# Unread bf16 matmuls on TensorE behind norms, between thin row scores and at the waits at the end of attentions

## The chip, the cores and the metric

The kernel runs on one core of one Trainium2 chip. The metric is the device time of one execution in microseconds (us); smaller is better. The engines are TensorE (PE, matmul), VectorE (DVE), ScalarE (ACT), GpSimd (POOL) and SyncE (SP). They run side by side, each through its own list in order, and wait for one another by semaphores.

## What is computed

A stack of four levels on x (4 sequences of 512 tokens, 128 features), with a context of 77 tokens of 64 features. Each level adds a gated cross attention and a gated feed-forward part:

```python
x = x + tanh(g_xattn[0]) * L0_xattn(layernorm(x), ctx)   # 16 heads of 8
x = x + tanh(g_ffn[0])   * L0_ffn(layernorm(x))          # quantised MLP
x = x + tanh(g_xattn[1]) * L1_xattn(layernorm(x), ctx)   # self attention a1, cross attention a2, 16 heads of 32, an MLP behind each
x = x + tanh(g_ffn[1])   * L1_ffn(layernorm(x))          # causal self attention, 16 heads of 8, then 8 experts, one per token
x = x + tanh(g_xattn[2]) * L2_xattn(layernorm(x), ctx)   # one head
x = x + tanh(g_ffn[2])   * L2_ffn(layernorm(x))          # 4 experts, two per token
x = x + tanh(g_xattn[3]) * L3_xattn(layernorm(x), ctx)   # 16 heads of 8
x = x + tanh(g_ffn[3])   * L3_ffn(layernorm(x))          # attention over the 4 sequences, 8 experts
```

## The kernel before

Everything stands transposed: features on the 128 partitions, tokens along the free side. All levels but the last feed-forward part run in a loop of two turns (`TURNS`), and a turn treats two sequences, u = 0 and 1, at the same time. Matmuls are f32 but for a few in bf16; they write the 8 banks of PSUM (`PSB[b]`, 512 f32 columns each). Each engine has one hand-written list. `TENSOR.did(...)` counts a step of PE and `pe.wait_ge(*VECTOR[...])` waits for one of DVE; PE takes its matmuls strictly in the order written. So a matmul that waits holds up all behind it, and one that does not wait delays what stands behind it by its own length, unless that would have waited anyway.

Three functions of PE's list are touched.

`norm(tag, src, ready)` normalises over features. PE centres u = 0 and 1 (line 613), ACT squares both (L1555), PE takes the means (line 616), ACT makes the reciprocal deviation with Ln and Exp (L1558, L1560), DVE multiplies (L1879) and in most cases applies gain and offset (L1884). PE then waits for DVE. The tags in order of a turn are l0x, l1o, l1a, l1b, a1n3, l1c, l1d, a2n3, l1f, l1g, l2x, l2f, l3x.

`cross(tag, dh)` is the cross attention, with dh = 8 in l0x and l3x and dh = 32 in a2. First come eight pairs of row scores of u = 0 (`rowscores`, line 641: 32 of the 128 rows of the array each), each followed by a maximum on DVE (L1927), in a ring of three pairs of banks. The maxima are turned (line 654), then columns of scores (line 670), exponentials on ACT (L1574) and values (line 695) of both sequences are interleaved. With dh = 8 the end is `heads` (line 709: sums per head), a reciprocal on DVE, `inverses` (line 719), and behind it the output projection (`linear`, line 1002).

`attend_past` is the causal attention of l1f, in 32 pieces of four heads. It starts with row scores (line 881, with `diagonals`, line 887) of pieces 0 to 4, the suffix sums (line 918) and the turned maxima. The loop over m then does row scores of piece m + 6, column scores (line 912) of piece m and values (line 932) of piece m - 2. Towards the end PE spreads small tables (`spread_out`, line 953), sums per head (`heads`, line 945), takes the logits of the router (`logits`, line 1206), and the experts follow (lines 1236 and 1242, with DVE L2391 between them). For u = 1 the queries are made by ACT (L1743, step `"l1f q", 1`); in the kernel before PE waits for it only ahead of column score 1 and row score 16.

Of the kernel before, what the change touches and what calls it, by code (L numbers as in the profile page):

```python
# [116 lines left out]
def program(nc, xT, ctxT, const, packs, l2w, w1, w2, out, tables):  # L117
    ctx = ExitStack()
    with ctx:
# [7 lines left out]
        PSB = [ps[:, b, :] for b in range(8)]  # L127
# [7 lines left out]
        def aux(u):  # L135
            return PSB[6 + u]
# [17 lines left out]
        identb = sb("identb", [128, 128], BF16)  # L154
        w1q = sb("w1q", [128, 512], BF16)
# [60 lines left out]
        SCALAR = Steps(sem("scalar_steps"), tables[1])  # L216
# [390 lines left out]
        def _(pe):  # L607
            ident = K["ident"]

            def norm(tag, src, ready, dim=128):  # L610
                for u in U:
                    pe.wait_ge(*ready(u))
                    pe.matmul(lin(u), K["centre"], src(u), start=True, stop=True).then_inc(*TENSOR.did(tag, "c", u))  # L613
                for u in U:
                    pe.wait_ge(*SCALAR[tag, "sq", u])
                    pe.matmul(aux(u), K["mean"], sq[:, u, :], start=True, stop=True).then_inc(*TENSOR.did(tag, "v", u))

            def cross(tag, dh):

# [10 lines left out]
                def rowscores(u, a):  # L630
                    i, hf = a // 2, a % 2
                    x = cplace("R", u, a)
                    free(x)
                    if a == 0:
                        pe.wait_ge(*VECTOR[tag, "kv", u])
                        pe.wait_ge(*VECTOR[tag, "q", u])
                    for b in (0, 1):
                        c = 2 * hf + b
                        at = slice(32 * c, 32 * c + 32)
                        if dh == 8:  # L640
                            mm = pe.matmul(PSB[cbank(x) + b][:, 0:4 * KC], qT[at, u, 0, 128 * i:128 * i + 128],  # L641
                                           kt[at, u].rearrange("p k t -> p (k t)"), start=True, stop=True,
                                           tile_position=(32 * c, 0))
                        else:
                            mm = pe.matmul(PSB[cbank(x) + b][:, 0:4 * KC], qT[:, u, c, 128 * i:128 * i + 128],
                                           apart(u)[:, c], start=True, stop=True)
                    mm.then_inc(*TENSOR.did(tag, "R", u, a))

                def turned(u):
                    x = cplace("turned", u)  # L650
                    pe.wait_ge(*VECTOR[tag, "cut", u])
                    free(x)
                    for i in range(4):
                        mm = pe.transpose(PSB[cbank(x)].bitcast(BF16)[:, 128 * i:128 * i + 128],
                                          cut[:, i].rearrange("p c r -> p (c r)"), identb[:])
                    mm.then_inc(*TENSOR.did(tag, "turned", u))
# [43 lines left out]
                def heads(u, hf):  # L700

                    x = 34 + u
                    if hf == 0:
                        free_late(x)
                    pe.wait_ge(*SCALAR[tag, "kept", u, hf])
                    to = PSB[cbank(x)][:, 0:64].rearrange("p (i c k) -> p i c k", i=4, c=4)
                    source = (xn if hf == 0 else sq)[:, u, :]
                    for i in range(4):
                        mm = pe.matmul(to[:, i, :, 2 * hf:2 * hf + 2], source[:, 128 * i:128 * i + 128],
                                       eighths[:, :, 1 - hf, :], start=True, stop=True, skip_group_check=True)  # L710
                    mm.then_inc(*TENSOR.did(tag, "heads", u, hf))
# [4 lines left out]
                def inverses(u):  # L716
                    pe.wait_ge(*VECTOR[tag, "inv", u])
                    for i in range(4):
                        mm = pe.matmul(PSB[cbank(34 + u) + 1][:, 128 * i:128 * i + 128], rs[:, u, 128 * i:128 * i + 128], ident,
                                       start=True, stop=True)  # L720
                    mm.then_inc(*TENSOR.did(tag, "inverses", u))
# [2 lines left out]

                for a in range(8):
                    rowscores(0, a)
                turned(0)
                for a in range(8):
                    colscores(0, a)
# [17 lines left out]
                if dh == 8:  # L747
                    heads(1, 0)
                    inverses(0)
                    heads(1, 1)  # L750
                    inverses(1)
                    return
                for u in U:
                    pe.wait_ge(*VECTOR[tag, "inv", u])
                    for k in range(4):
# [3 lines left out]
                        for c in range(4):  # L759
# [3 lines left out]
                                           stop=True, tile_position=(0, 32 * c))  # L763
# [100 lines left out]
            def attend_past(token_values, logits):  # L864
# [19 lines left out]
                def diagonals(p, h):  # L884
                    x, lo = pplace(p, h), 128 * ktile_past(p)
                    for b in (0, 1):
                        mm = pe.matmul(PSB[pbank(x) + b][:, lo:lo + 128], identb[:], beyond[:], start=False, stop=True)  # L887
                    mm.then_inc(*TENSOR.did("l1f", "R", p, h))
# [49 lines left out]
                def heads(u, hf):  # L938

                    bank = 3 - 2 * u  # L940
                    pe.wait_ge(*(VECTOR["l1f", "raised", 7] if u == 0 else VECTOR["l1f", "later", 0]))
                    pe.wait_ge(*SCALAR["l1f", "kept", 2 * u + hf])
                    to = PSB[bank][:, 0:64].rearrange("p (i c k) -> p i c k", i=4, c=4)
                    for i in range(4):
                        mm = pe.matmul(to[:, i, :, 2 * hf:2 * hf + 2], kept_sums(2 * u + hf)[:, 128 * i:128 * i + 128],
                                       eighths[:, :, 1 - hf, :], start=True, stop=True, skip_group_check=True)
                    mm.then_inc(*TENSOR.did("l1f", "heads", u, hf))

                def spread_out(tag, u, bank):

                    pe.wait_ge(*VECTOR["l1f", tag, u])
                    for i in range(4):
                        mm = pe.matmul(PSB[bank][:, 128 * i:128 * i + 128], xn[:, u, 128 * i:128 * i + 128], ident, start=True,
                                       stop=True)
                    mm.then_inc(*TENSOR.did("l1f", tag, u))

                for p in range(5):
                    for c in range(4):
                        rowscore(p, c)
                        if c % 2:  # L960
                            diagonals(p, c // 2)
                    if p == 0:
                        token_values(1)
                for u in U:
# [6 lines left out]
                for m in range(34):  # L971
                    if m % 4 == 3 and m < 28:
                        turned((m + 1) // 4)
                    for g in range(4):
                        if g == 2 and m >= 2:
                            values(m - 2)
                        if m + 6 < 32:
                            rowscore(m + 6, g)
                        if m < 32:
                            colscore(m, g)  # L980
                        if m + 6 < 32 and g % 2:
                            diagonals(m + 6, g // 2)
                    if m == 28:
                        pe.wait_ge(*VECTOR["l1f", "max", 31, 1])
                        spread_out("e0", 0, 1)
                    if m == 29:
                        spread_out("e0", 1, 2)
                        heads(0, 0)
                        heads(0, 1)
                    if m == 31:  # L990
                        spread_out("inv", 0, 4)
                    if m == 32:
                        heads(1, 0)
                heads(1, 1)
                logits(0)
                spread_out("inv", 1, 2)

            def linear(tag, w, src, ready, rows=None):
                for u in U:
# [91 lines left out]
            with pe.Fori(0, TURNS) as t:  # L1091
# [110 lines left out]
                def logits(u):  # L1202
                    pe.wait_ge(*VECTOR["l1f o", u])
                    pe.wait_ge(*SCALAR["l1f", "exp", 31, 3])
                    for i in range(4):
                        mm = pe.matmul(aux(u)[:, 16 * i:16 * i + E1], x2[:, u, 128 * i:128 * i + 128], w["Wsw"],
                                       start=True, stop=True)
                    mm.then_inc(*TENSOR.did("l1f logits", u))
# [92 lines left out]
                for u in U:  # L1301
# [3 lines left out]
                    for c in range(2):  # L1305
                        mm = pe.matmul(scb(2 * u + c), w["rW1"][:, 128 * c:128 * c + 128], xn[:, u, :], start=True,
                                       stop=True)
# [38 lines left out]
                for u in U:  # L1346
                    pe.wait_ge(*VECTOR["l2f cwT", u])
                    pe.wait_ge(*VECTOR["l2f out", 2 * E2 - 2 + u])
                    for i in range(4):
                        pe.matmul(aux(u)[:, 128 * i:128 * i + 128], x2[:, u, 128 * i:128 * i + 128], ident, start=True,  # L1350
                                  stop=False)
# [1409 lines left out]
```

## Time and profile before

| | |
|---|---|
| median of 3 runs | 1945.53 us (1936.75 to 1956.92) |
| profiled execution | 1932.59 us, of which the span of the trace is 1930.5 us |
| mean granted TensorE clock | 0.87 of 2.4 GHz |
| busy: PE, DVE, ACT, POOL | 1643.6, 880.0, 715.9, 146.9 us |
| share of the chain that ended last: PE, DVE, ACT | 78%, 12%, 7% |
| DMA | 30.17 MB, 16 GB/s on average |

PE's clock is granted at one of two levels, 2.4 GHz (1.00) or 1.2 GHz (0.50); a value between them is a mean over a stretch that has both. "Idle before" of a PE row counts from the modelled end of the last matmul.

### The profile page before, as it was taken

The page shows a single profiled execution, that of the slowest core. Times are in us where ns is not written, and L with a number is a line of the kernel's source. Part 1 is how long each engine was busy: PE and PEld are TensorE (multiplying, and loading weights), DVE is VectorE, ACT ScalarE, POOL GpSimd, SP SyncE. Part 2 cuts the span into 40 slices and gives each one's busy share as a digit, 9 for nine tenths or more (in the row PEclk, how much of TensorE's full clock was granted, in tenths as well). Part 3 has the DMA queues.
Part 4 walks back from the last instruction along what each step waited for, and adds up shares of the span by engine and source line. Part 5 has one row for each costly group of instructions (what it writes and reads, how often), then busy time and mean ns, then how long its engine had stood idle before and what let it go on. Part 6 is the DMA issues. An engine that isn't in the chain of part 4 may idle for free.

```text
span 1930.5 us, 22528 instructions
## 1 busy us (share of the span) xinstructions
PE 1643.6 (85%) x9068; PEld 762.3 (39%) x9068; DVE 880.0 (46%) x1746; ACT 715.9 (37%) x1267; POOL 146.9 (8%) x207
## 2 busy tenths in 40 slices
PE   5748999989899989997648999989899989988487
PEld 2323333332344536633323323332343436543274
DVE  4474664253456353324474663353456352337312
ACT  2333455324435225232332455323445125243133
POOL 0000011100012000000000111100012000002232
PEclk9768899989989699956768999989999689889688
DMA  4000000000000100000000000000000100002241
GB/s 178 1 1 0 1 2 1 1 1 1 0 1 1 44 1 1 1 1 2 1 1 0 1 1 1 0 1 1 0 1 2 44 1 1 1 33 44 62 135 59
DMA packets 18107, 30.17 MB, mean 16 GB/s; under 512 B 4640, under 2 KB 12640, under 8 KB 17104
## 3 DMA queue, kind: packets, MB, share of 16 engines
q1 hardware_dynamic: 16752, 26.10, 4.2%
q0 software_dynamic: 1248, 2.59, 0.4%
q8 instruction: 74, 1.21, 0.3%
q14 instruction: 33, 0.27, 0.0%
HBM read 23.49 MB, written 5.19 MB: 15 GB/s over the span
## 4 chain that ended last, share of the span: by engine, by line
PE 78%; DVE 12%; ACT 7%; issue 2%; DMA 1%; SPq 0%; POOL 0%; POOLq 0%; DVEq 0%; ACTq 0%
PE ps L783 8%; PE ps L881 5%; PE ps L670 5%; PE ps L613 3%; PE ps L815 3%; PE ps L1323 3%; PE ps L1335 3%; PE ps L1020 3%; PE ps L695 3%; PE ps L1012 3%; PE ps L932 2%; PE ps L829 2%; PE ps L1242 2%; PE ps L912 2%; PE ps L804 2%
## 5 line engine op out<-in xcount | busy, mean ns | idle before, releaser
L2000 DVE TENSOR_REDUCE peak<-ps 128x1 f32<-128x512 f32 x256 | 165.4, 686 | 119.0 <-PE ps L783 118.4
L1620 ACT ACTIVATE big<-ps 128x512 f32<-128x512 f32 x256 | 139.6, 595 | 133.8 <-PE ps L806 126.9
L783 PE MATMUL ps<-pp,qT 32*128 32x512 f32 x512 | 169.5, 714 | 3.5 <-DVE peak L2000 2.1
L804 PE MATMUL ps<-qT,pp 32*128 32x512 f32 x512 | 160.4, 649 | 0.0
L1641 ACT ACTIVATE big<-ps 128x512 f32<-128x512 f32 (+3 forms) x256 | 100.3, 436 | 112.5 <-PE ps L912 111.7
L2037 DVE TENSOR_REDUCE crest<-ps 128x2 f32<-128x512 f32 (+3 forms) x128 | 105.2, 825 | 65.7 <-PE ps L887 65.6
L1574 ACT ACTIVATE big<-ps 77x1024 f32<-77x1024 f32 x96 | 94.7, 1019 | 95.8 <-PE ps L670 95.2
L912 PE MATMUL ps<-qT,pp 32*128 32x256 f32 (+3 forms) x512 | 124.4, 494 | 0.9 <-ACT big L1641 0.9
L1927 DVE TENSOR_REDUCE small<-ps 128x8 f32<-128x616 f32 x96 | 74.2, 797 | 102.8 <-PE ps L641 58.1
L881 PE MATMUL ps<-pp,qT 32*128 32x384 f32 (+3 forms) x512 | 109.2, 501 | 9.5 <-DVE crest L2037 8.5
L1555 ACT ACTIVATE sq<-ps 128x512 f32<-128x512 f32 x52 | 31.1, 597 | 204.4 <-PE ps L613 204.4
L670 PE MATMUL ps<-qT,kt 32*77 32x512 f32 x384 | 94.1, 741 | 9.8 <-ACT spare L1565 9.6
L783 PEld LDWEIGHTS ps<-pp,qT 32*128 32x128 f32 x512 | 59.2, 202 | 83.4 <-DVE peak L2000 65.9
L542 POOL TENSOR_SCALAR_AFFINE_SELECT big<-big 128x512 f32<-128x512 f32 x64 | 40.8, 637 | 616.4 <-PE ps L815 616.4
L560 POOL TENSOR_SCALAR_AFFINE_SELECT big<-big 128x512 f32<-128x512 f32 x64 | 40.8, 637 | 555.9 <-ACT big L1641 555.9
L1879 DVE TENSOR_TENSOR xn<-ps,rs 128x512 f32<-128x512 f32 x40 | 27.7, 692 | 94.0 <-ACT rs L1560 94.0
L815 PE MATMUL ps<-big,cst 128*32 128x512 f32 x512 | 68.1, 604 | 0.0
L1012 PE MATMUL ps<-xn,w_l 128*128 128x512 f32 x96 | 51.7, 699 | 18.1 <-DVE xn L1884 18.1
L1778 ACT ACTIVATE big<-ps,w_l 128x512 f32<-128x512 f32 x64 | 44.0, 687 | 59.1 <-PE ps L1323 57.5
L695 PE MATMUL ps<-big,vx 77*32 77x512 f32 x384 | 58.3, 690 | 6.0 <-ACT qT L1586 6.0
L1335 PEld LDWEIGHTS ps<-pt,big 128*128 128x128 f32 x512 | 59.4, 192 | 6.7 <-issue 6.7
L806 PE MATMUL ps<-spare,minus 32*128 32x512 bf16 x256 | 61.4, 377 | 0.0
(484 smaller groups left out, 2775.3 us busy)
## 6 DMA issues: line engine op xcount, KB each, us to landing
big<-in_w SPq DMA_DIRECT2D x23, 256.0 KB
pt<-in_l2w SPq DMA_DIRECT2D x2, 2048.0 KB, 7.5
w_l<-in_l SPq DMA_DIRECT2D x1, 3086.0 KB, 17.3
pp<-in_w SPq DMA_DIRECT2D x1, 2048.0 KB, 9.6
big<-by_expert SPq DMA_DIRECT2D x23, 66.0 KB, 2.0
by_expert<-cst SPq DMA_DIRECT2D x1, 1472.0 KB, 16.3
cst<-in_const SPq DMA_DIRECT2D x1, 1298.0 KB, 5.8
w_l<-in_l SPq DMA_DIRECT2D x1, 1218.0 KB, 8.0
```

The lines of the kernel that those rows point to most:

```text
L670: mm = pe.matmul(PSB[cbank(x) + b][0:KC, :], keys, query, start=not less, stop=less, tile_position=(32 * c, 0))
L695: mm = pe.matmul(PSB[k // 2 if dh == 8 else 0][32 * c:32 * c + 32, :], vx[:, u, at:at + 32], cprob(u, k)[:, c, :], start=dh == 32 or k % 2 ...
L783: pe.matmul(rbank(x), qT[at, u, k, 128 * i:128 * i + 128], keyT(u, k)[at, :], start=True, stop=True, tile_position=(32 * c, 0)).then_inc(* ...
L804: pe.matmul(tbank(y), keyT(u, k)[at, 128 * j:128 * j + 128], qT[at, u, k, :], start=True, stop=False, tile_position=(32 * c, 0))
L815: mm = pe.matmul(PSB[1][32 * c:32 * c + 32, :], K["col8"][:, 128 * k + 32 * c:128 * k + 32 * c + 32], prob(n)[:, c, :], start=n % 16 == 0, ...
L881: pe.matmul(PSB[pbank(x) + c % 2][:, 0:hi], qT[at, u, k, 128 * i:128 * i + 128], keyT(u, k)[at, 0:hi], start=True, stop=False, tile_positi ...
L912: pe.matmul(tbank(y)[:, lo:512], keyT(u, k)[at, 128 * j:128 * j + 128], qT[at, u, k, lo:512], start=True, stop=True, tile_position=(32 * c ...
L1012: pe.matmul(scb(c), w[:, 128 * c:128 * c + 128], src(u), start=True, stop=True)\
L1335: mm = pe.matmul(lin(u)[:, 128 * i:128 * i + 128], hid[u][:, c, 128 * i:128 * i + 128], W2[:, 128 * c:128 * c + 128], start=c == 0, stop=c ...
L1620: A(prob(m)[:, TURN_OF[g], :], tbank(tplace(m, g)), ACT.Exp).then_inc(*SCALAR.did("a1", "exp", m, g))
L2000: v.tensor_reduce(peak[:, p // 4 % 2, i, c:c + 1], rbank(ring(p, c)), AX.X, ALU.max)\
L2037: v.tensor_reduce(crest[:, u, i, 2 * h:2 * h + 2, k], ps[:, b:b + 2, 0:hi], AX.X, ALU.max)\
```

## The change

PE gets matmuls whose result nobody reads: `identb` (bf16, 128 x 128) is the stationary operand and `w1q` (bf16, 128 x 512) streams, into a bank that is free there. They count no step. There are 114 per turn, 228 in all: 48 behind the means of eight norms, 16 between the row scores of u = 0 in l0x and l3x, 20 at the ends of these two, and 30 in l1f. One wait is new: in the row scores of pieces 1 to 4 of l1f, PE waits for ACT's queries of u = 1, because these are read from bank 6, which the added matmuls overwrite.

```diff
+            def busy(b, n):
+                for _ in range(n):
+                    pe.matmul(PSB[b], identb[:], w1q[:], start=True, stop=True)
             def norm(tag, src, ready, dim=128):
...
                     pe.matmul(aux(u), K["mean"], sq[:, u, :], ...).then_inc(*TENSOR.did(tag, "v", u))
+                if tag not in ("l0x", "l1c", "l2x", "l2f", "l3x"):
+                    busy(5, 6)
...
                 for a in range(8):                 # cross
                     rowscores(0, a)
+                    if dh == 8:
+                        busy(0, 1)
...
                     heads(1, 0)
                     inverses(0)
                     heads(1, 1)
+                    busy(2, 6)
                     inverses(1)
+                    busy(2, 4)
                     return
...
                         rowscore(p, c)             # attend_past, p in 0..4
                         if c % 2:
                             diagonals(p, c // 2)
+                            if p:
+                                pe.wait_ge(*SCALAR["l1f q", 1])
+                                busy(6, 1)
...
                     if m == 29:
+                        busy(4, 6)
                         spread_out("e0", 1, 2)
...
+                busy(5, 6)
                 heads(1, 1)
+                busy(5, 6)
                 logits(0)
                 spread_out("inv", 1, 2)
+                busy(5, 4)
```

## Rows read from the trace of the kernel before

**Rows 1.** The page: span, granted clock by slice, chain by engine.
```profile
span 1930.5 us, 22528 instructions
...
PEclk9768899989989699956768999989999689889688
...
PE 78%; DVE 12%; ACT 7%; issue 2%; DMA 1%; SPq 0%; POOL 0%; POOLq 0%; DVEq 0%; ACTq 0%
```

**Rows 2.** Busy time, clock (PEclk) and DMA in six stretches, all engines.
```profile
824.20:868.00 43.80, 42.64 (x212) 14.72 (x212) 8.75 (x14) 17.93 (x20) 0.00 (x0) 0.57 0.00 1
...
1687.60:1719.00 31.40, 28.91 (x212) 10.93 (x212) 9.17 (x15) 17.50 (x20) 0.00 (x0) 0.93 0.00 1
...
370.00:376.80 6.80, 5.74 (x7) 2.52 (x8) 1.52 (x3) 2.59 (x4) 0.00 (x0) 0.50 0.00 0
...
639.60:653.30 13.70, 13.23 (x62) 8.37 (x60) 4.11 (x8) 2.21 (x8) 1.27 (x2) 0.50 0.00 1
...
656.70:677.20 20.50, 20.13 (x58) 9.61 (x57) 10.18 (x33) 1.52 (x4) 0.00 (x0) 0.50 0.22 93
...
530.40:540.70 10.30, 10.30 (x33) 4.25 (x32) 5.41 (x9) 0.00 (x0) 0.00 (x0) 0.50 0.01 2
```

**Rows 3.** Timeline, PE behind norms: start, us, work; idle before in brackets.
```profile
141.10 2.36 PE L613 MATMUL ps<-xn,cst 128*128 128x512 f32 x4 [1.31 <-DVE xn L1879]
...
148.30 3.57 PE L613 MATMUL ps<-x,cst 128*128 128x512 f32 x4 [3.03 <-DVE x L1884]
...
157.97 5.37 PE L1151 MATMUL ps<-xn,w_l 128*128 128x512 f32 x8 [4.29 <-DVE xn L1884]
...
163.18 3.60 PE L1156 MATMUL ps<-x,w_l 128*128 128x512 f32 x8
...
371.06 9.97 PE L1012 MATMUL ps<-xn,w_l 128*128 128x512 f32 x16 [3.03 <-DVE xn L1884]
...
407.93 8.60 PE L1012 MATMUL ps<-xn,w_l 128*128 128x512 f32 x16 [3.02 <-DVE xn L1884]
...
498.04 7.13 PE L1012 MATMUL ps<-xn,w_l 128*128 128x512 f32 x16 [3.03 <-DVE xn L1884]
```

**Rows 4.** Timeline, PE in the experts of l1f, low and full clock.
```profile
665.73 0.60 PE L1236 MATMUL ps<-xn,identb 8*128 8x512 bf16 x1
...
668.27 0.60 PE L1236 MATMUL ps<-xn,identb 8*128 8x512 bf16 x1
...
688.09 0.39 PE L1236 MATMUL ps<-xn,identb 8*128 8x512 bf16 x1
...
689.46 0.39 PE L1236 MATMUL ps<-xn,identb 8*128 8x512 bf16 x1
```

**Rows 5.** Timeline, PE at the end of the attention of l1f.
```profile
639.07 1.58 PE L953 MATMUL ps<-cst,xn 128*128 128x128 f32 x8 [1.66 <-DVE xn L2072]
...
656.17 1.35 PE L945 MATMUL ps<-cst,rs 128*128 128x8 f32 x8 [0.81 <-ACT rs L1646]
...
657.38 1.85 PE L1206 MATMUL ps<-w_l1f,x 128*128 128x8 f32 x8
```

**Rows 6.** Timeline, ACT and PE at the start of that attention.
```profile
525.95 2.83 ACT L1743 ACTIVATE qT<-ps,bqm,part_scaled 128x512 f32<-128x512 f32 x4
...
528.19 1.13 PE L881 MATMUL ps<-pp,qT 32*128 32x512 f32 x4 [0.63 <-DVE crest L2037]
...
530.90 1.65 PE L881 MATMUL ps<-pp,qT 32*128 32x384 f32 x4
```

**Rows 7.** Timeline, DVE and PE in l3x: row scores, then the end.
```profile
816.52 5.74 DVE L1927 TENSOR_REDUCE small<-ps 128x8 f32<-128x616 f32 x8
...
817.37 3.92 PE L641 MATMUL ps<-kt,qT 32*128 32x308 f32 x20 [0.38 <-DVE small L1927]
...
874.27 2.08 PE L719 MATMUL ps<-cst,rs 128*128 128x128 f32 x8 [1.11 <-DVE rs L1956]
...
876.14 3.09 PE L1002 MATMUL ps<-xn,w_l 128*128 128x512 f32 x4
```

## The prediction

> **What bounds the kernel now.** I read the page first. The chain that ended last is 78% PE, 12% DVE and 7% ACT [rows 1], so PE is the bound in most stages, and DMA is nowhere in it. The clock line has digits from 5 to 9 all along the span: a mean of 0.87 means that about 26% of 1930.5 us, some 500 us, ran at 1.2 GHz. Then I read the busy time of stretches where the clock is low [rows 2]. In 639.6 to 653.3, 656.7 to 677.2 and 530.4 to 540.7 us PE has work nearly all the time at 0.50, so each us there holds half of what it could. The same work at both levels shows the price: 212 matmuls of l3x take 43.8 us at 0.57 in the first turn and 31.4 us at 0.93 in the second [rows 2]. Last I read the timeline around the gaps of PE. Behind the norm l1a it is idle for 3.03 us and comes back at half clock: four pieces (an f32 matmul stands in the trace as two) take 3.57 us, where eight take 3.60 us at full clock [rows 3]. The reader is to see three kinds of added matmul: some fill a wait of PE that exists anyway, some stand directly ahead of work that is ready, and some come with a new wait.
>
> **Price of one.** No row shows the same matmul 128 rows high at full clock. The nearest is L1236, also 512 bf16 columns, on 8 rows: 0.60 us at low and 0.39 us at full clock [rows 4]. The difference of 0.21 us is the streaming time at full clock, if it doubles at half clock; so one costs 0.21 us or 0.43 us of PE in a series, and six cost 1.28 or 2.56 us. Its weight load should overlap; if it does not, the bounds are the whole durations, 0.39 and 0.60 us.
>
> **Norms (96 matmuls).** All eight norms make PE wait: 1.31 us where DVE applies no gain (l1o, l1f), about 3.03 us where it does, 4.29 us in l1b [rows 3]. Six at full clock take 1.28 us, so they are free; at low clock they overrun only the two short gaps, by 1.25 us each. I take +0.5 us in all. The gain is the work behind the gap at full clock. l1a: 3.57 us for four pieces becomes 1.8 to 1.9 (0.45 us per piece), -1.7, in the first turn only. l1b: 5.37 against 3.60 us, -1.8 in both turns [rows 3]; but 3.0 us of idle remain behind the six, as much as let the clock fall elsewhere, so I take half: -1.8. a1n3: the 16 pieces take 9.97 us against 7.13 us for the same group in a2n3, -2.8, twice. l1d: 8.60 against 7.13 us, -1.5, twice [rows 3]. l1g: not shown in a row; sized like l1a and taken by half, -1.7 for both turns. Sum -13.8. The ends are 0 and -19.
>
> **End of the attention of l1f (44).** The first six fill a wait of 1.66 us for the table e0 [rows 5], at no cost. Two stretches at low clock follow [rows 2]. In the second, the experts come at 2.54 us each (668.27 - 665.73) and at 1.37 us at full clock (689.46 - 688.09) [rows 4]: five of them -5.9, two sets of logits of 1.85 us [rows 5] -1.8, three L1236 of 0.21 us -0.6. The first stretch has 13.23 us of PE [rows 2]; half of it would be 6.6, but exponentials and masks pace part and matmuls of 8 columns, bound by weights, may not hold the clock, so I take a third, -2.2. Costs: six ahead of `heads(1, 1)` have only 0.81 us of cover, +0.5; six ahead of `logits(0)` have none, because the logits are ready, +1.3, and behind them wait the routing on DVE, the hot rows and the first expert; four behind `spread_out("inv", 1, 2)`, up to +0.85. Net -7.9 per turn, -16. The ends: if nothing is held and all run at low clock, the three groups cost 1.75 + 2.56 + 1.71 = 6.0 us per turn; if the first stretch is held too, -12.
>
> **Start of that attention (16) and the new wait.** ACT ends the queries of u = 1 at 525.95 + 2.83 = 528.78 us. PE now stands in front of the second half of piece 1, done before 528.19 us, with all row scores, `suffix`, `turned(0)` and so the first exponentials queued behind it; DVE waits for the maxima. A pair and its maximum come behind the wait, so piece 2 starts some 1.5 us later than at 528.19 [rows 6]. The matmuls add 0.21 or 0.43 us to each pair, with little cover: a pair of 512 columns took 1.13 us at full and one of 384 took 1.65 us at half clock [rows 6], and PE sets the pace in the latter. The clock is low from 530.4 to 540.7 us [rows 2]; if held, some 5 us come back (the suffix matmuls 3, the thin ones 2). I give this one chance in three, because the new wait is itself a gap: 1.5 + 2.2 - 1.7 = +2, twice, +4. The ends are -2 and +4.5 each.
>
> **Row scores in l0x and l3x (32).** DVE sets the pace: 5.74 us for eight maxima, 0.72 each. The PE row says the same: idle for 0.38 us before a maximum frees a bank [rows 7]. A pair of 308 columns needs about 0.54 us at full clock (308/512 of 0.90), with one more 0.75 us: 0.03 over, 1 us in all 32, which the ring of three pairs lets PE absorb. Behind the last there is still a wait for the cut, the turned maxima and ACT until the column scores, which nothing fills, and the clock was below full in the column scores of both turns of l3x [rows 2]. If it held, the first turn of l3x would give 12.4 us [rows 2]; the three others, if they stand like the second turn at 0.93, some 2 to 3 us each. I take one chance in four of 20, -5. The Trainium skill (TensorE: Matmul & The Clock Gate, section Why this matters for your kernels) blames idle gaps between bursts for drops. By that alone nothing placed in waits of 0.4 us could matter and this term would be 0. The trace speaks against idle time as the whole cause: PE was busy 42.64 of 43.80 us in l3x and the clock stayed mostly low [rows 2].
>
> **Ends of l0x and l3x (40).** Six have 1.11 us of cover in front of `inverses(1)`; four stand ahead of the output projection, whose first half is ready [rows 7]. At full clock that costs 0.2 + 0.85 = 1.0 us, at low clock 1.45 + 1.71 = 3.2 us; part comes back where the projection runs faster, whose four pieces took 3.09 us [rows 7] against 1.8 at full clock. I take +1.0, four times, +4.
>
> **The sum.** -13.8 + 0.5 - 16 + 4 - 5 + 4 = -26.3 us. The profiled execution took 1932.59 us, 2.1 more than its span, and would become 1906. The median of the runs is 12.9 us above it; I put that on both kernels: 1919.
>
> **The rivals.** (1) The clock holds in the cross attentions and at the start of l1f as well: 15 us more there and 7 more in l1f than taken, about 1897. For it: the same cross attention ran at 0.93 once. Against: the wait ahead of the column scores is unfilled. (2) The falls only move: with other gaps left (l1c, l0f, the wait ahead of the column scores), the clock falls a little later and half of the gross gain goes (43 us: 13.8 norms, 21 and 3.3 in l1f, 5 row scores), while 17 us of costs stay: -4, 1941. For it: l1c has no filler and l1d follows directly. (3) Slower: at places where the clock is low already the matmuls run at half clock and are not covered. The place is the three ends and the new wait: 4 x 3.2 + 2 x 6.0 + 2 x 4.5 = 34 us, less 13.8 of the norms, +20: 1966. It decides from the point where low clock meets PE at those places; below 13 us of it, the gains win. For it: the projection of l3x [rows 7] and the end of l1f's attention [rows 2] run at low clock now. Against: the matmuls themselves are work that can bring the clock back. (4) They do not move the clock at all, since their operands are bf16 and unread: only the costs at today's levels: 12.8 at the ends, 9.6 and 7.4 in l1f, 0.5, so 1976.
>
> **How the numbers follow.** Chances: forecast 0.47 (its own range 1908 to 1931), rival (1) 0.15, (2) 0.27, (3) 0.06, (4) 0.05. A measurement here can tell about 1%, 19 us, from no change: faster is below 1926, slower above 1965. Faster: 0.40 of the forecast's 0.47, 0.14 of (1) and 0.03 of (2), 0.57. Slower: half of (3) and all of (4), 0.08. The rest 0.35. The range leaves out half of (1) at the lower side and (3) and (4) at the upper: 1897 to 1946.
>
> **What would show it.** In the new profile: mean clock from 0.87 to about 0.91; the group behind a1n3 near 7.1 us in both turns; experts at 1.37 us from the first on; the idle time ahead of row scores of piece 1 or 2 of l1f grown to some 1.5 us; the row scores of l3x still at 0.72 us. I am wrong if the clock line shows as many low digits as now, if the experts still come at 2.54 us, or if PE's idle time behind norms becomes overrun instead of filled.

## The result and the profile after

| | before | after |
|---|---|---|
| median, same chip | 1951.22 us (4 runs, 1936.75 to 1978.95) | 1973.68 us (4 runs, 1969.84 to 1994.02) |
| ratio | | 1.0219, 95% interval 1.0157 to 1.028 |
| profiled execution | 1932.59 us | 1970.67 us |

The kernel became slower, by 22 us in the median and 38.1 us from profile to profile. The prediction was 1919 with a range of 1897 to 1946. A ratio, here and below, leaves out runs over 1.5% above the fastest of a kernel (of the kernel before up to 12 of 17), and the two such executions that were profiled are ordinary ones in which more stages were slow, so the median of all runs stands beside each. The page of the kernel after, the lines that answer to [rows 1]:

```profile
span 1968.5 us, 22984 instructions
...
PEclk9569799997989888967859799999989989869788
...
PE 79%; DVE 10%; ACT 7%; issue 2%; DMA 1%; POOL 1%; SPq 0%; POOLq 0%; DVEq 0%; ACTq 0%
```

The chain and the mean clock (0.868) are those of before; the low digits have moved, not gone. To find where 38 us went, I took the start of the same DVE instruction in both traces at the borders of each stage. This gives a ledger, in us:

| stage (turn 1, turn 2) | before | after | difference |
|---|---|---|---|
| l0x, with its ends | 52.7, 52.5 | 69.3, 50.2 | +16.6, -2.3 |
| up to a1n3's linears | 20.2, 20.4 | 17.4, 17.4 | -2.8, -3.0 |
| l1d, up to a2's maxima | 14.4, 14.0 | 11.9, 11.2 | -2.5, -2.8 |
| a2 | 64.5, 63.6 | 77.3, 63.8 | +12.8, +0.2 |
| start of l1f's attention | 26.1, 26.7 | 32.3, 33.1 | +6.2, +6.4 |
| its end, with the first expert | 58.8, 58.1 | 63.7, 48.2 | +4.9, -9.9 |
| l3x, with its ends | 64.3, 49.7 | 66.4, 64.4 | +2.1, +14.7 |

Three entries are larger than all others: a cross attention that takes 13 to 17 us longer. One of them, a2, has no added matmul inside. The busy table of the stretch from the first to the last exponential of each cross attention (columns: stretch, us, busy of PE, PEld, DVE, ACT, POOL, the clock, DMA), in the order l0x, a2, l3x of turn 1, then of turn 2. First before:

```profile
44.10:71.90 27.80, 25.59 (x189) 9.41 (x183) 7.98 (x12) 17.08 (x20) 0.00 (x0) 0.91 0.00 1
429.90:470.60 40.70, 37.24 (x230) 12.47 (x230) 10.20 (x11) 19.36 (x24) 0.00 (x0) 1.00 0.00 0
826.70:866.10 39.40, 38.25 (x188) 12.21 (x183) 7.98 (x12) 17.40 (x20) 0.00 (x0) 0.56 0.00 1
907.90:938.30 30.40, 28.56 (x189) 10.22 (x184) 7.98 (x12) 17.19 (x20) 0.00 (x0) 0.81 0.01 1
1293.30:1334.10 40.80, 37.33 (x231) 12.56 (x230) 10.20 (x11) 19.42 (x24) 0.00 (x0) 1.00 0.00 0
1690.10:1716.80 26.70, 24.26 (x189) 8.55 (x184) 7.98 (x12) 17.04 (x20) 0.00 (x0) 0.98 0.01 1
```

Then after:

```profile
46.30:88.00 41.70, 40.38 (x184) 11.80 (x177) 7.97 (x12) 17.35 (x20) 0.00 (x0) 0.51 0.00 0
441.60:492.70 51.10, 48.54 (x230) 15.37 (x230) 10.20 (x11) 19.33 (x24) 0.00 (x0) 0.77 0.00 1
862.60:903.10 40.50, 39.35 (x190) 12.22 (x184) 7.97 (x12) 17.43 (x20) 0.00 (x0) 0.54 0.00 0
945.30:972.10 26.80, 24.60 (x189) 8.97 (x184) 7.97 (x12) 17.13 (x20) 0.00 (x0) 0.96 0.00 1
1321.50:1362.20 40.70, 37.29 (x230) 12.52 (x230) 10.20 (x11) 19.36 (x24) 0.00 (x0) 1.00 0.00 1
1715.80:1756.30 40.50, 39.35 (x190) 12.15 (x184) 7.97 (x12) 17.39 (x20) 0.00 (x0) 0.54 0.00 0
```

Mostly, a cross attention is either short (26 to 30 us in l0x and l3x, 41 in a2) at a clock near full, or long (39 to 42, and 51; later also 55) at a lower one. DVE and ACT do the same work in the same busy time; PE has 40.38 us of busy time for what it does in 25.59 at the higher clock. Before has one long of six, after has four. The six stretches sum to 205.8 and 241.3 us: 35.5 of the 38.1 us are here, and everything else in the change comes to about +3.

How a long one begins is in PE's timeline of l0x, turn 1, of the kernel after (start, us, work, idle time before it in brackets):

```profile
34.34 0.79 PE L648 MATMUL ps<-kt,qT 32*128 32x308 f32 x4
35.06 0.39 PE L613 MATMUL ps<-w1q,identb 128*128 128x512 bf16 x1
35.38 0.79 PE L648 MATMUL ps<-kt,qT 32*128 32x308 f32 x4
...
42.34 0.39 PE L613 MATMUL ps<-w1q,identb 128*128 128x512 bf16 x1
43.82 0.40 PE L661 MATMUL ps<-identb,spare 128*128 128x128 bf16 x4 [1.09 <-DVE spare L1953]
44.99 1.16 PE L677 MATMUL ps<-qT,kt 32*77 32x512 f32 x6 [0.78 <-ACT spare L1583]
```

The row scores with their added matmuls run at full clock. Then PE waits for the cut (1.09 us) and for the shift (0.78 us), with 0.40 us of transposes between. The change fills neither wait. PE's busy time and clock in that stretch:

```profile
43.00:45.00 2.00, 0.40 (x5) 1.00 0.00 0
45.00:47.00 2.00, 2.00 (x16) 0.83 0.04 8
47.00:88.00 41.00, 39.68 (x180) 0.51 0.00 0
```

The clock falls right behind these waits and stays at 1.2 GHz for 41 us, although PE is busy for 39.68 of them. The two long l3x begin the same way; the long a2 (turn 1) is at 0.50 from its start to about 459 us and mostly full from there. In the kernel before the waits are there too (1.84 and 0.78 us), and in l0x of turn 1 the clock falls behind them but is back after 7 us:

```profile
42.00:49.00 7.00, 6.92 (x34) 0.52 0.01 2
49.00:73.00 24.00, 21.87 (x178) 1.00 0.00 1
```

In l3x of turn 1 of before, the long one, it falls earlier, at 820.6 us, while PE still takes the row scores. It stays low through both waits and the column scores:

```profile
813.30:820.50 7.20, 6.62 (x34) 1.00 0.00 0
...
822.80:861.50 38.70, 36.75 (x164) 0.50 0.00 0
```

So a long cross attention is one whose column scores start at the low clock, or fall to it at once, and stay there. The fall itself comes in or behind the two waits, or already in the row scores.

### The profile page after: what moved, and what is told of

Same layout as the page of the kernel before. It is cut to its first block, busy times and chain, and to the rows that moved or that the text cites. A ratio compares the mean times of both kernels' runs of the same rounds, so it can differ in the third digit from the quotient of the medians.

```text
span 1968.5 us, 22984 instructions
## 1 busy us (share of the span) xinstructions
PE 1711.2 (87%) x9296; PEld 776.3 (39%) x9296; DVE 881.4 (45%) x1746; ACT 716.7 (36%) x1267; POOL 146.5 (7%) x207
## 4 chain that ended last, share of the span: by engine, by line
PE 79%; DVE 10%; ACT 7%; issue 2%; DMA 1%; POOL 1%; SPq 0%; POOLq 0%; DVEq 0%; ACTq 0%
PE ps L794 7%; PE ps L677 5%; PE ps L892 5%; PE ps L702 3%; PE ps L826 3%; PE ps L1341 3%; PE ps L618 3%; PE ps L1353 3%; PE ps L1038 3%; PE ps L943 2%; PE ps L613 2%; PE ps L648 2%; PE ps L1030 2%; PE ps L840 2%; PE ps L652 2%; PE ps L815 2%
## 5 line engine op out<-in xcount | busy, mean ns | idle before, releaser
L677 PE MATMUL ps<-qT,kt 32*77 32x512 f32 x384 | 106.5, 844 | 9.7 <-ACT spare L1583 9.6
L542 POOL TENSOR_SCALAR_AFFINE_SELECT big<-big 128x512 f32<-128x512 f32 x64 | 40.7, 636 | 628.7 <-PE ps L826 628.7
L560 POOL TENSOR_SCALAR_AFFINE_SELECT big<-big 128x512 f32<-128x512 f32 x64 | 40.7, 636 | 561.5 <-ACT big L1659 561.5
L613 PE MATMUL ps<-w1q,identb 128*128 128x512 bf16 x228 | 75.7, 445 | 3.8 <-ACT qT L1761 3.8
L702 PE MATMUL ps<-big,vx 77*32 77x512 f32 x384 | 69.8, 817 | 5.1 <-ACT qT L1604 5.1
L648 PE MATMUL ps<-kt,qT 32*128 32x308 f32 x256 | 63.2, 577 | 2.4 <-ACT big L1592 1.5
```

The source lines that it names most:

```text
L613: pe.matmul(PSB[b], identb[:], w1q[:], start=True, stop=True)
L677: mm = pe.matmul(PSB[cbank(x) + b][0:KC, :], keys, query, start=not less, stop=less, tile_position=(32 * c, 0))
L702: mm = pe.matmul(PSB[k // 2 if dh == 8 else 0][32 * c:32 * c + 32, :], vx[:, u, at:at + 32], cprob(u, k)[:, c, :], start=dh == 32 or k % 2 ...
```

## The experiments

Two theories stand in the first four expectations. T: the matmuls among the row scores cost time on the path and leave the clock low in the cross attentions. R: the clock there falls and returns by chance. A third, which I call W, came out of these four and is tested behind them: what decides is the two waits ahead of the column scores, which the change left unfilled, and filling them keeps every cross attention short.

The experiments add or leave out only unread matmuls and the new wait. In each of the three groups the kernel before ran on the same chip.

**Parts alone and taken away.** Four kernels; before on this chip: 1932.42 us, median of 11 (1923.12 to 1989.58).

`u1_no_row_fill`, the kernel after without the matmuls among the row scores:
```diff
                     rowscores(0, a)
-                    if dh == 8:
-                        busy(0, 1)
```


> The changed kernel without the 32 matmuls between the row scores of l0x and l3x. Theory T (they cost on the path and leave the clock low in the cross attention): the profile of the changed kernel shows 1.04 us per row score with one of them behind it, where DVE's pace was 0.72, so 8 x 0.32 = 2.6 us per cross attention, 10 us in all, and the low clock in l0x and l3x (43 to 53 us from the first column score to the heads, against 31 at full clock) goes back to what it was before: 1970 - 10 - 20 to 25 = 1937 to 1942. Rival R (the clock in the cross attentions falls and returns by chance): only the 10 us come back, 1960, and the profile still has one or two of the four cross attentions above 40 us.

`u2_no_new_wait`, the kernel after without the new wait and its matmuls:
```diff
-                            if p:
-                                pe.wait_ge(*SCALAR["l1f q", 1])
-                                busy(6, 1)
```


> The changed kernel without the new wait and the 8 matmuls at the start of the attention of l1f. Between the same two instructions of DVE the changed kernel is 6.3 us later than the one before in each turn. Both theories: 12 to 13 us come back, 1958 to 1962, and the stretch at low clock there (530 to 541 us before) stays as it was before. If the wait were hidden and the lag came only from the clock, less than 5 us.

`o1_norms_only`, the kernel before plus only this:
```diff
+                if tag not in ("l0x", "l1c", "l2x", "l2f", "l3x"):
+                    busy(5, 6)
```


> The kernel before with the 48 matmuls per turn behind the means of eight norms, and nothing else of the change. Theory T: these are the part that pays, 2.8 us behind a1n3, 2 behind l1d, 1 behind l1a and l1b in each turn as the changed kernel's trace shows, 12 to 14 us in all: ratio to before 0.993. Rival R: the same direct gain, but the clock in the cross attentions moves by chance, so that the runs scatter by 10 to 20 us around it as those of the kernel before do.

`o2_row_fill_only`, the kernel before plus only this:
```diff
                     rowscores(0, a)
+                    if dh == 8:
+                        busy(0, 1)
```


> The kernel before with the 32 matmuls between row scores of l0x and l3x alone. Theory T: 10 us on the path and 20 to 25 us of low clock in l0x and l3x: ratio to before 1.015 to 1.018, and the four cross attentions (first column score to the first heads of u = 1) take 40 us or more in most of the four. Rival R: only the 10 us, 1.005, and the four cross attentions take between 31 and 45 us as before.

Measured, with the length of the six cross attentions read as above (order l0x, a2, l3x of turn 1, then of turn 2; long ones bold). The profile of before and all numbers of after are those of the comparison above:

| kernel | median (range) | profiled | us from first to last exponential |
|---|---|---|---|
| before | 1932.42 (1923.12 to 1989.58) | 1932.59 | 27.8, 40.7, **39.4**, 30.4, 40.8, 26.7 |
| after | 1973.68 (1969.84 to 1994.02) | 1970.67 | **41.7**, **51.1**, **40.5**, 26.8, 40.7, **40.5** |
| no row fill | 1977.11 (1941.91 to 1999.34) | 1999.31 | **41.7**, **50.9**, **41.7**, **41.7**, **50.9**, **41.7** |
| no new wait | 1949.73 (1943.47 to 1957.47) | 1943.47 | 26.2, **51.2**, **40.5**, 27.8, **50.9**, 27.8 |
| norms only | 1948.1 (1939.31 to 1976.18) | 1939.31 | 26.7, 40.7, **39.5**, 30.4, **51.0**, 26.6 |
| row fill only | 1976.75 (1946.64 to 2018.03) | 1989.25 | 26.8, **51.0**, **40.6**, **41.6**, **55.2**, **41.6** |

No kernel did what a sum of parts would give. Without the row fills T wanted 1937 to 1942 us and R 1960; the profiled one came out 29 us slower than the kernel after, with six long ones. The row fills alone did what T said of them (ratio 1.0145, three of the four at 40 us or more), but both a2 turned long too, where there is no row fill. Without the new wait 12 to 13 us were to come back, and 24 did in the median and 27 in the profile. The norms alone saved 10 us up to the attention of l1f in turn 1 and came out 7 us slower than before, since a2 of turn 2 turned long; nothing was added inside it, and this is its row against 40.8 us in before:

```profile
1283.80:1334.80 51.00, 47.51 (x230) 15.38 (x230) 10.20 (x11) 19.43 (x24) 0.00 (x0) 0.79 0.00 1
```

Long ones are what moves the times most, and neither T nor a sum of parts tells where they come. In l0x and l3x they are as frequent with row fills (7 of 12 profiled in after, no new wait and row fill only) as without (8 of 16 in before, no row fill, norms only and `w1_wait_only` below). The next kernels fill the waits.

**Filling the two waits.** Before on this chip: 1947.89 us, median of 17 (1912.38 to 1987.84).

`f1_gap_fill`, the kernel before plus, in all six cross attentions:
```diff
                 for a in range(8):
                     rowscores(0, a)
+                busy(1, 8 if dh == 8 else 6)
                 turned(0)
+                busy(1, 3)
```


> The kernel before plus matmuls in the two waits ahead of the column scores of every cross attention: 8 (6 in a2) behind the last row score, 3 behind the transposes; none anywhere else. The theory: the clock falls in these two waits (1.84 and 0.78 us without a matmul in l0x and l3x, 1.40 and 0.78 in a2), and whether it falls decides if a cross takes 27 or 41 us (41 or 51 in a2). Then all six crosses take the short time wherever the kernel enters them at the full clock. From the profile of before (one long cross of six) that gives 1932.6 - 13 = 1920 profiled, and the median goes by how many are long in an average execution of before: ratio 0.985 to 1.0, with less scatter than 1923 to 1990. The rival, that a cross is long or short by chance whatever fills its waits (the column scores themselves let the clock fall): still one to four long crosses, ratio 1.00 +- 0.01, scatter as before.

`f2_gap_norms`, that and the six behind the norms, as in the kernel after:

> The filled waits ahead of the column scores and six matmuls behind the norms. The norms alone gave about 10 us in turn 1 and 7 in turn 2 directly, and their kernel came out 1.3% slower because crosses turned long. If filled waits keep the crosses short, the direct gain stays: profiled about 1932.6 - 13 - 15 = 1905, ratio 0.98 to 0.99. The rival (crosses long by chance): ratio 1.00 to 1.015, as the norms alone.

`f3_gap_norms_end`, that and, at the end of l1f's attention:
```diff
                     if m == 29:
+                        busy(4, 6)
                         spread_out("e0", 1, 2)
...
+                busy(5, 6)
                 heads(1, 1)
+                busy(5, 6)
                 logits(0)
                 spread_out("inv", 1, 2)
+                busy(5, 4)
```


> The same with the matmuls at the end of l1f's attention (6 ahead of the spreads, 6 and 6 around the last heads, 4 behind the last inverses) too. In the kernel after, these held the clock in turn 2 (that stretch took 48 us instead of 58) and not in turn 1 (64 instead of 59). Theory: it stays one of these two in each turn, so 0 to -20 us beside the kernel with gaps and norms, -5 on average: ratio 0.975 to 0.99. The rival: nothing gained, +5, ratio 0.985 to 1.01.

`w1_wait_only`, the kernel before plus only the new wait, without a matmul:
```diff
                             diagonals(p, c // 2)
+                            if p:
+                                pe.wait_ge(*SCALAR["l1f q", 1])
```


> The kernel before plus only the new wait at the start of l1f's attention, without its matmuls. In the kernel after, the stretch at the start of l1f took 6.3 us more in both turns, predicted 2. If the wait itself costs it (ScalarE reaches the copy of q late, and the clock falls in the 1.92 us without work), this kernel loses 3 to 6 us in each turn at that place; if the matmuls cost it (each pair with its matmul at the low clock), under 1 us.

**And the halves.** Before on this chip: 1944.87 us, median of 19 (1916.7 to 1982.18).

`g1_after_and_gaps`: the kernel after, whole, with the two `busy` lines of `f1_gap_fill`.

> The kernel after, whole, plus the matmuls in the two waits ahead of the column scores of every cross attention. If what made the change lose is that the clock fell in these unfilled waits (four long crosses instead of one), all six are short here, those of l0x and l3x at 26 plus about 2.5 us for the row fills, and the profiled time falls from 1970.7 by about 14 + 10 + 14 + 14 = 52 to about 1920; against before the median ratio is 0.975 to 0.99, and the scatter is that of the gap kernels (1%), not 3%. The rival, that the added matmuls themselves keep the clock down in the crosses: still three or four long ones, over 1950.

`p1_first_gap` (only the line ahead of `turned(0)`) and `p2_second_gap` (only the one behind it), on the kernel before.

> Before plus only the 8 (6) matmuls behind the last row score; the wait of 0.78 us behind the transposes is left. If the longer wait decides, no cross turns long: 1915 to 1925 as with both. If any wait without a matmul is enough while the clock is on the edge, one or two long ones: 1930 to 1950.

> Before plus only the 3 matmuls behind the transposes; the wait of 1.84 us ahead of them is left. If the longer wait decides, long crosses as in before: median 1935 to 1955 with its scatter. If the wait right ahead of the column scores decides, all short: 1915 to 1925.

`f4_gap_norms_end_less`: `f3_gap_norms_end` without `busy(4, 6)`.

> The kernel with gaps, norms and ends of l1f's attention, without the 6 matmuls ahead of the spreads (e0). They took 0.45 us each at the low clock where the clock was down already. If they only cost, this is 1 to 3 us a turn faster: 1884 to 1888. If they bring the clock back earlier, it is 5 to 15 us slower: 1894 to 1904.

| kernel | median (range, runs) | ratio, 95% | profiled | six cross attentions, us |
|---|---|---|---|---|
| gaps | 1918.13 (1907.48 to 1923.65, 12) | 0.9938 [0.9897, 0.9979] | 1919.83 | 26.1, 40.7, 26.1, 26.2, 42.1, 26.1 |
| gaps, norms | 1904.63 (1895.94 to 1909.08, 6) | 0.9874 [0.9806, 0.9941] | 1905.87 | 26.2, 40.7, 26.1, 26.2, 41.8, 26.2 |
| gaps, norms, end | 1889.23 (1886.22 to 1893.04, 4) | 0.98 [0.9709, 0.9891] | 1891.05 | 26.2, 40.7, 26.1, 26.2, 42.0, 26.2 |
| wait only | 1 run | | 1970.52 | 27.8, 40.7, 27.8, **41.7**, **55.2**, **39.4** |
| after and gaps | 1902.64 (1901.66 to 1915.24, 4) | 0.9875 [0.9764, 0.9986] | 1901.66 | 26.2, 40.7, 26.2, 26.1, 40.7, 26.1 |
| first gap | 1923.63 (1908.01 to 1935.4, 10) | 0.9927 [0.988, 0.9974] | 1919.97 | 26.2, 40.8, 30.4, 26.2, 42.0, 26.1 |
| second gap | 1926.07 (1919.63 to 1935.69, 10) | 0.9988 [0.9943, 1.0034] | 1927.21 | 26.2, 40.7, 26.5, 26.2, 40.7, 26.2 |
| gaps, norms, less end | 1892.14 (1885.64 to 1904.66, 4) | 0.9819 [0.9697, 0.9941] | 1886.48 | 26.2, 40.7, 26.2, 26.2, 40.7, 26.1 |

With filled waits no profiled cross attention is long, in seven kernels with one or both fills: 42 of 42 are short, against 18 of 42 in the seven profiles without. One, l3x of turn 1 in `p1_first_gap`, took 30.4 us. Two rows of `f1_gap_fill`, l0x of turn 1 and a2 of turn 2, the only one of the six that still has low clock:

```profile
43.90:70.00 26.10, 23.38 (x189) 8.58 (x181) 7.98 (x12) 16.93 (x20) 0.00 (x0) 1.00 0.00 1
...
1272.50:1314.60 42.10, 38.88 (x230) 12.77 (x230) 10.20 (x11) 19.43 (x24) 0.00 (x0) 0.96 0.00 1
```

This is not because the clock no longer falls. In six of the seven kernels, all but `g1_after_and_gaps`, the row scores of l0x and l3x have no fill, and the clock went low in them in 20 of 24 profiled cases. It was back before the first exponential, or 0.5 us behind it, in all but the one of 30.4 us. PE's busy time and clock in l3x of turn 1 of `f1_gap_fill` (column scores from 825.03 us), then in l0x of turn 1 of `p2_second_gap` (column scores from some 42 us):

```profile
818.30:825.00 6.70, 6.70 (x21) 0.50 0.00 0
825.00:852.50 27.50, 24.79 (x198) 1.00 0.00 1
...
37.10:43.80 6.70, 5.07 (x24) 0.50 0.00 0
43.90:70.40 26.50, 23.78 (x194) 1.00 0.01 1
```

So the fills do two things: they prevent a fall in the waits (as in `g1_after_and_gaps` below, against the kernel after), and they go with an early return from one that came before. Theory W had only the first.

The decisive one is `g1_after_and_gaps`. It has every matmul and the wait of the kernel after, plus 62 more matmuls, and is 71.0 us faster in the median (on another chip), 69.0 in the profile, of which 55.3 are in the six stretches (186.0 against 241.3 us); I had expected about 50. Its timeline at the same place, then PE's busy time and clock:

```profile
41.87 2.12 PE L613 MATMUL ps<-w1q,identb 128*128 128x512 bf16 x9
43.82 0.39 PE L661 MATMUL ps<-identb,spare 128*128 128x128 bf16 x4
44.04 0.81 PE L613 MATMUL ps<-w1q,identb 128*128 128x512 bf16 x3
44.98 1.16 PE L677 MATMUL ps<-qT,kt 32*77 32x512 f32 x6
```
```profile
43.00:45.00 2.00, 1.87 (x14) 1.00 0.00 0
45.00:47.00 2.00, 1.80 (x16) 1.00 0.03 8
47.00:75.00 28.00, 25.48 (x202) 1.00 0.00 1
```

The transposes start at 43.82 us and the column scores at 44.98, as in the kernel after (43.82 and 44.99): these matmuls cost nothing on the path. Theories T and R both fall. The matmuls of the change do not keep the clock low once the waits are filled, and a cross attention is then not long by chance: 12 runs of `f1_gap_fill` lie within 16 us, 17 of before within 75. Either fill alone keeps all six profiled ones from turning long, but gives less: 21.2 and 18.8 us under the median of before, where both give 29.8 on another chip, and the ratio of the second, 0.9988, can't be told from 1. Neither wait alone decides. What I had expected of the second if the longer wait decides (long ones as in before) did not come, though only 3 matmuls were added in a wait of 0.78 us.

`w1_wait_only` was meant for the start of l1f. With no added matmul anywhere it has three long ones and took 1970.52 us, as much as the kernel after. It is one execution, and 6 of 51 of before lie there too, so it shows only that long ones need no added matmul.

The fastest version is `f3_gap_norms_end`: 1889.23 us, 58.7 under the median of before on the same chip (by the ratio 2.0% faster, interval 1.1 to 2.9) and 84.5 under the kernel after, on another.

## Why the prediction was wrong

**The failed step is the cross attentions.** I wrote that behind the last row score a wait is left "which nothing fills", and that this was a chance of one in four to gain 20 us. In the sum this is the term of -5, and no term was above 0 for a cross attention that turns long. Read rightly, the same sentence was the risk: five of the six stood short in one profiled execution, in front of an unfilled wait, and could all turn long. I priced a possible return of one and no loss of the others; the runs showed +35.5 us in these six stretches. Each costs 10.4 us (a2) to 13.9 (l0x), and the profile after had three more. It was there to be seen in the runs of before, which spread over 20 us in three runs and over 77 in all 51 (1912.38 to 1989.58). I took the 12.9 us between profile and median for something to add to both kernels; it is about the price of one more long cross attention, but the other executions have no trace, so this is an estimate.

**Rival (2)** ("the falls only move") was the nearest in kind, with 1941, but it let the gains be lost only where I had counted gains. None of my rivals had a stage lose that the change does not touch. In number rival (4), 1976, and rival (3), 1966, came nearest to 1973.68, and that is luck. (4) has matmuls that do not move the clock at all, but a1n3's group went from 9.97 to 7.13 us; (3) has all its 34 us of cost at the three ends and the new wait, where the kernel after lost 12.6 at the start of l1f's attention and gained 5.0 at its end.

The other terms can be checked apart from this, on kernels whose cross attentions are held. In medians, with profiled differences in brackets; g1 ran on another chip than f1 and f3, with a median of before 3.0 us lower:

| term | predicted | measured |
|---|---|---|
| norms | -13.3 | -13.5 (-14.0), f2 - f1 |
| end of l1f's attention | -16 | -15.4 (-14.8), f3 - f2 |
| row scores, ends of l0x and l3x, new wait | +3 | +13.4 (+10.6), g1 - f3 |
| all | -26.3 | -15.5 (-18.2), g1 - f1 |

By stage, the third row is not the row scores. From f1 to g1 the start of l1f's attention takes 12.0 us more in both turns together, and l0x and l3x 0.1 less; f3 has some 8 us less than f1 and f2 at that start, and nothing in f3 accounts for it.

**Norms: right in sum.** In the kernel after, a1n3's group and that behind l1b:

```profile
172.66 5.35 PE L1169 MATMUL ps<-xn,w_l 128*128 128x512 f32 x8 [3.09 <-DVE xn L1902]
...
386.93 7.13 PE L1030 MATMUL ps<-xn,w_l 128*128 128x512 f32 x16 [1.73 <-DVE xn L1902]
```

The second is 9.97 us in before and 7.13 now, as predicted [rows 3]. The first stayed at 5.35 against 5.37 us: six matmuls leave 3.09 us of idle time there, and the clock falls all the same, the case for which I had taken half. The ledger has more behind l1d than I took, 2.5 and 2.8 us against 1.5.

**Price of one: right in a series.** Six hold up what stands behind them by 1.30 us at full clock (1547.26 to 1548.56 in the kernel after) and by 2.53 at low (682.79 to 685.32), against 1.28 and 2.56 predicted. Between two pairs of row scores one costs 0.32 us, not 0.21.

**Row scores: mis-sized.** I had a pair at 0.54 us and pair plus added matmul at 0.75, hidden behind DVE's 0.72. In the rows above pairs start every 1.04 us: 0.72 for the pair and 0.32 for the added one. My 0.54 was scaled by columns from matmuls of 512, and no row showed that this holds. The row itself said otherwise: twenty pieces in 3.92 us [rows 7] are five pairs of 0.78, so PE was as much the bound as DVE. DVE now waits for PE between its maxima:

```profile
35.18 0.80 DVE L1945 TENSOR_REDUCE small<-ps 128x8 f32<-128x616 f32 x1
36.22 0.80 DVE L1945 TENSOR_REDUCE small<-ps 128x8 f32<-128x616 f32 x1 [0.24 <-PE ps L648]
```

That is 8 x 0.32 = 2.6 us in each of four cross attentions, +10 where I had 0. Where the cross attentions are held, l0x and l3x as a whole took no longer, so as much came back elsewhere in them, their ends included, which I had at +1 each; two errors cancel here: l0x took 49.2 and 49.5 us in `g1_after_and_gaps` against 46.5 and 48.3 in `f1_gap_fill`, l3x 49.2 and 47.3 against 51.0 and 49.5, in sum -0.1 us. In the first l0x of g1 the clock stayed at 1.00 through the end and the projection.

**Start of l1f's attention: mis-sized.** Predicted +2 per turn, inside bounds of -2 to +4.5; measured +6.2 and +6.4. PE of the kernel after:

```profile
551.05 0.39 PE L613 MATMUL ps<-w1q,identb 128*128 128x512 bf16 x1 [1.92 <-ACT qT L1761]
...
554.94 0.63 PE L613 MATMUL ps<-w1q,identb 128*128 128x512 bf16 x1
555.51 2.08 PE L892 MATMUL ps<-pp,qT 32*128 32x512 f32 x4
```
```profile
541.00:551.50 10.50, 8.22 (x45) 4.74 (x47) 8.24 (x18) 8.37 (x13) 0.00 (x0) 1.00 0.00 0
551.50:562.00 10.50, 10.50 (x32) 3.23 (x32) 3.83 (x4) 0.00 (x0) 0.00 (x0) 0.50 0.01 2
```

The wait is 1.92 us, and right behind it the clock falls, as it does in before without the wait [rows 2]; but it stays low for 17.1 us (551.3 to 568.4) where before has 10.2. The group of 512 columns that took 1.13 us in [rows 6] takes 2.08, and an added matmul 0.63. The wait alone (`w1_wait_only`) makes this stretch 28.9 and 29.7 us against 26.1 and 26.7: +2.8 and +3.0, where I had 1.5. The other 3.4 are the eight matmuls: at the low clock two groups of 512 columns start 2.76 us apart in the kernel after and 2.33 with the wait alone, 0.43 more each, where I had 2.2 in all. And the 1.7 that I took off for a held clock did not come.

**End of l1f's attention: right in sum, not in kind.** I had -7.9 in each turn. PE in that stretch of the kernel after, turn 1 and 2:

```profile
666.70:730.40 63.70, 61.85 (x246) 0.71 0.09 34
1536.20:1584.40 48.20, 45.62 (x244) 0.96 0.12 44
```

In turn 2 the clock held nearly throughout (before: 58.1 us), in turn 1 the added matmuls were paid at the low clock (2.72 and 2.74 us for six) and gave nothing. I took this for one of two outcomes, held or not, and so did my expectation for f3; but f3 took 56.4 and 59.0 us there (clock 0.82 and 0.77) and f4 52.6 in turn 2 (0.87), so it comes in shares as well. Over all profiles the stretch from the same DVE instruction to the same one took 57.3 to 63.5 us without these matmuls (16 stretches) and 46.6 to 63.0 with all or most of them (12), 60.5 and 54.5 on average. With held cross attentions it took 56.4 and 55.7 us in g1 and 64.2 and 63.5 in f1, which has no matmul there: -7.8 each, the size I had. But f1's own stretches are 5.4 us longer than those of before, with the same work: here a fall did move to a later place, as rival (2) has it. And f3 - f2 is not all from here: the ends give -7.8 and -1.0 us, while 4.0 us in each turn are gained at the start of the attention, where that kernel adds nothing; the cause of these is not shown. Of the six ahead of the spread of e0, `f4_gap_norms_end_less` settles nothing: 2.9 us slower without them in the median (on another chip), 4.6 faster in the profile, with ranges that overlap.

The signs that I had named for being wrong came as well: the clock line has as many low digits as before and a mean of 0.868, not 0.91, and the row scores are at 1.04 us, not 0.72.

**What stays open.** Which cross attention turns long in a given execution. The kernels with row fills have high medians (1976.75 alone, 1973.68 in the kernel after), but so has the one without them (1977.11), and the wait alone reached 1970.52. All four runs of the kernel after lie at 1969.84 us or more and 6 of 51 of before do, so the change as a whole does make slow executions likelier; which part of it does, or whether any small shift in time would, was not settled. What brings the clock back early in some cross attentions and not in others isn't shown either, nor how few matmuls are enough.

## What to carry to other kernels

If executions of one kernel spread by several per cent and its profile shows the same stage once short and once long, read the clock there first, and count every stage of that kind as a risk, also those that the change does not touch. Fill the waits directly ahead of work that can stay at the low clock for long once it is there, with matmuls that end before the wait does: here 62 of them gave 30 us in the median and cut the spread from 75 to 16 us, and with these in place the 228 elsewhere gave half of that. A matmul between two others that run back to back is paid (here 0.32 us each), even where the engine behind them seems to set the pace.

## What the runs showed of the hardware

In l0x of turn 1 of the kernel after PE stayed at 1.2 GHz through 41 us in which it was busy for 39.68: the f32 column scores and row scores on 32 rows of the array, and the bf16 ones between them, did not bring 2.4 GHz back, while at full clock the same work kept it with PE busy for 25.48 of 28 us. It is no fixed rule: in before the same work was back at full clock after 7 us. Behind eight added matmuls of 128 rows and 512 columns the clock was back before the column scores began (825.0 us in `f1_gap_fill`), in a place where before stayed low for 41 us (820.6 to 861.5). The Trainium skill (TensorE: Matmul & The Clock Gate, section Why this matters for your kernels) puts drops down to idle gaps between bursts. I had used these busy stretches against it. For the fall in the kernel after these runs agree with it: it came behind waits of 1.09 and 0.78 us and was absent when they were filled. But single waits here are short, a fall came also at the end of 7.2 us with PE busy for 6.62, and idle gaps do not account for how long the clock then stays low.

The same kernel takes 1912 to 1988 us on one chip. The Trainium skill (TensorE: Matmul & The Clock Gate, section What's actually happening) says that the number of slow matmuls of one kernel varies from run to run, and puts the penalty of the ramp at under 1% of a typical kernel's span. The first agrees in kind with these runs, in which the time of one kernel varies by 4%. The second isn't enough to reckon with here: where the clock stays low behind a fall, each costs 10 to 14 us of some 1930, up to six times.
